# Graph attention on one core: a turn's keys and masks in one transfer each, and a ring of fourteen quads instead of fifteen

## The reference

```python
x_src, x_dst = x[src], x[dst]
for r in range(5):
    mask = edge_types == r
    q = einsum('eh,khd->ekd', x_dst, W_Q[r])      # 100000 x 8 x 16
    k = einsum('eh,khd->ekd', x_src, W_K[r])
    v = einsum('eh,khd->ekd', x_src, W_V[r])
    logits = (q * k).sum(-1) / scale + attn_bias[r]
    # softmax over the edges of this type with the same dst
    attn = segment_softmax(where(mask, logits, NEG), dst)
    out += segment_sum(attn[:, :, None] * v, dst)
out = out @ out_proj_w.T + out_proj_b
h = layernorm(out + x) * ln_gamma + ln_beta
return layernorm(x + h)
```

## Time and profile before

| | us |
|---|---|
| median of 3 runs | 1296.82 (1294.86 to 1297.39) |
| profiled execution, from first to last instruction | 1301.8 |
| DVE busy | 1002.1 (77%) |
| PE busy | 938.5 (72%) |
| POOL busy | 763.0 (59%) |
| ACT busy | 547.3 (42%) |
| mean granted clock of PE, share of full speed | 0.546 |
| DMA | 209.26 MB, mean 161 GB/s |

### The profile page before, as it was taken

How to read it: one execution, slowest core, us unless ns; L and a number is a source line. 1 busy time by engine, 2 the same in 40 slices (tenths; PEclk the granted TensorE clock), 3 DMA queues, 4 the chain that set the end, 5 groups by cost and what they waited for, 6 DMA issues and landing times.

```text
span 1301.8 us, 19088 instructions
## 1 busy us (share of the span) xinstructions
PE 938.5 (72%) x5180; PEld 827.1 (64%) x5180; DVE 1002.1 (77%) x1851; ACT 547.3 (42%) x1044; POOL 763.0 (59%) x859
## 2 busy tenths in 40 slices
PE   9924467866778767877787776877677677666777
PEld 4513456765667656766676765767576666666677
DVE  3656678877878778878878788887788788778996
ACT  5624443444434444444444444444444334343322
POOL 0067666666666666666666666666666666666640
PEclk9956555555555555555555555555555555555555
DMA  8976555554655555555654555655555455555410
GB/s 318 379 216 180 168 159 172 157 160 144 166 159 156 148 157 167 157 139 166 174 161 145 146 164 157 182 140 152 162 168 148 136 140 155 146 141 154 131 48 12
DMA packets 121376, 209.26 MB, mean 161 GB/s; under 512 B 22845, under 2 KB 79546, under 8 KB 121166
## 3 DMA queue, kind: packets, MB, share of 16 engines
q0 software_dynamic: 37632, 102.81, 27.8%
q1 hardware_dynamic: 79602, 92.61, 23.8%
q10 hardware_dynamic: 4032, 12.57, 2.5%
HBM read 176.92 MB, written 30.99 MB: 160 GB/s over the span
## 4 chain that ended last, share of the span: by engine, by line
DVE 36%; issue 28%; another core or an unknown queue 16%; PE 14%; ACT 2%; DVEq 2%; DMA 1%; ACTq 0%; POOL 0%; POOLq 0%; SPq 0%
DVE LT L1324 6%; DVE pool L1416 4%; PE pp L1863 4%; DVE av L666 4%; DVE pool L1387 4%; DVE pool L1288 3%; PE pp L572 3%; DVE pool L1310 2%; PE pp L1807 2%; DVE Tt L1300 2%; DVE Yt L1373 2%; DVE ohn L650 2%; PE pp L1846 2%; DVE Mt L1402 2%
## 5 line engine op out<-in xcount | busy, mean ns | idle before, releaser
L1699 POOL DMA_INDIRECT ring<-KVtab,kvi x784 | 745.6, 951 | 491.0 <-issue 207.3
L1807 PE MATMUL pp<-qwin,pool 128*128 128x128 bf16 x2352 | 293.5, 309 | 73.5 <-issue 53.4
L1863 PE MATMUL pp<-ohn,av 128*128 128x32 f32 x1464 | 328.1, 392 | 20.6 <-issue 18.5
L1863 PEld LDWEIGHTS pp<-ohn,av 128*128 128x128 f32 x1464 | 324.4, 328 | 22.1 <-issue 18.7
L1807 PEld LDWEIGHTS pp<-qwin,pool 128*128 128x128 bf16 x2352 | 262.9, 151 | 112.9 <-issue 111.4
L1310 DVE TENSOR_TENSOR pool<-pp,ring 128x512 f32<-128x512 f32 x196 | 133.5, 681 | 81.9 <-remote 67.3
L909 ACT ACTIVATE Et<-pool 120x512 f32<-120x512 f32 (+1 forms) x66 | 41.6, 630 | 293.2 <-DVE pool L1288 160.5
L1884 PE MATMUL pp<-pool,negb 128*128 128x512 bf16 (+1 forms) x84 | 37.3, 444 | 169.2 <-ACT pool L897 107.4
L882 ACT ACTIVATE pool<-rkb,npid 128x512 bf16<-128x512 bf16 x196 | 139.4, 711 | 36.2 <-DMA rkb<-Ktab 18.9
L1846 PEld LDWEIGHTS pp<-sel,pool 120*128 120x128 f32 (+1 forms) x536 | 129.5, 326 | 38.5 <-issue 38.4
L666 DVE TENSOR_TENSOR av<-ring,pp 128x512 f32<-128x512 f32 x183 | 124.2, 679 | 34.2 <-remote 34.0
(11 more groups left out here) (133 smaller groups left out, 969.1 us busy)
## 6 DMA issues: line engine op xcount, KB each, us to landing
rkb<-Ktab SPq DMA_DIRECT2D x196, 128.0 KB
mk<-Mtab SPq DMA_DIRECT2D x201, 100.2 KB
qwin<-Qfast SPq DMA_DIRECT2D x196, 96.0 KB
KVtab<-pool SPq DMA_DIRECT2D x25, 640.0 KB, 6.3
ring<-KVtab,kvi POOLq DMA_INDIRECT x784
Qfast<-pool ACTq DMA_DIRECT2D x21, 480.0 KB
Qfast<-ring SPq DMA_DIRECT2D x4, 480.0 KB
xs<-in_x_b SPq DMA_DIRECT2D x5, 320.0 KB
```

Of the source, the lines that this page charges most:

```text
L1699: e.indirect_dma_start(kv[:, home(m), j, :], None, KV, bass.IndirectOffsetOnAxis(kvi[:, 4 * q + j:4 * q + j + 1], 0)).then_inc(kv_in[m % 6 ...
L1807: last = e.matmul(pp[2 + m % 2][:, j * C:(j + 1) * C], ohr[:, m % OR, j * C:(j + 1) * C], qwin[:, m % 3, k * C:(k + 1) * C], start=(k == 0 ...
L1863: last = e.matmul(sums_at(f)[:, 0:n], weighed_at(f)[:, j, :], hot_at(f)[:, j, 0:n], start=(j == 0), stop=(j == 3))
```

## The change

- Keys: `load_keys(i)` fetches the rows of all quads of turn i in one transfer, into one of two buffers of three rows each (before: one row, one of three). It is issued in SP's step of the last quad of turn i-2 and waits until ACT has read that one (`KEYS_IN`). ACT waits for the turn's transfer.
- Masks: `load_masks(i)` fetches the masks of the three streams in one transfer. Its source has three dimensions, stream, 40 copies, and the row. All waits for masks count 16 instead of 48.
- The ring: `KR` is 14 instead of 15. Gathers wait for the weighing of quad m-14.
- `pad`, a temporary of the setup in the ring's space, shares its place with the first columns of `natd`, which has been read by then.

```diff
-KR = 15
+KR = 14
...
+def quads_of(i):
+    return [m for m in range(NQ) if turn_of(m)[0] == i]
+
+
+KEYS_IN = {quads_of(i - 2)[-1]: i for i in range(2, NW)}
...
-        pad = temp.take([2, 512], F32, HQ)
         differ = temp.take([2, MROW], F32, HQ)
         junk = natd.bitcast(F32)
+        pad = junk[:, :, 0:512]
...
-        rkb = sb("rkb", [128, 3, 512], BF16)
+        rkb = sb("rkb", [128, 2, G, 512], BF16)
...
-            def load_keys(m):
-                if m == 0:
+            def load_keys(i):
+                if i == 0:
                     e.wait_ge(rk_stored, 2 * 16)
-                if m >= 3:
-                    e.wait_ge(keys_dist, m - 2)
-                q = quad_of(m)
-                e.dma_start(rkb[:, m % 3, :], RK[q:q + 1, :].partition_broadcast(128)).then_inc(rk_in[m % 3], 16)
+                n = len(quads_of(i))
+                if i >= 2:
+                    e.wait_ge(keys_dist, quads_of(i - 2)[-1] + 1)
+                e.dma_start(rkb[:, i % 2, 0:n, :],
+                            RK[i:i + (n - 1) * STREAM + 1:STREAM, :].partition_broadcast(128)).then_inc(rk_in[i % 2], 16)
...
-                for g in range(G):
-                    q = STREAM * g + i
-                    e.dma_start(mk[g * R * H:(g + 1) * R * H, i % MR, :, :].rearrange("p e k -> p (e k)"),
-                                MT[q:q + 1, :].partition_broadcast(R * H)).then_inc(mask_in[i % MR], 16)
+                e.dma_start(mk[:, i % MR, :, :].rearrange("p e k -> p (e k)"),
+                            MT[i:i + 2 * STREAM + 1:STREAM, None, :].broadcast_to([G, R * H, 2 * MROW])).then_inc(
+                                mask_in[i % MR], 16)
...
-            for m in range(3):
-                load_keys(m)
+            for i in range(2):
+                load_keys(i)
...
-                if s + 3 < NQ:
-                    load_keys(s + 3)
+                if s in KEYS_IN:
+                    load_keys(KEYS_IN[s])
...
             def keys(m):
-                e.wait_ge(rk_in[m % 3], 16 * (m // 3 + 1))
+                i, g = turn_of(m)
+                e.wait_ge(rk_in[i % 2], 16 * (i // 2 + 1))
...
-                e.activation(ab[:, :], rkb[:, m % 3, :], ACT.Abs, bias=npid[:, 0:1]).then_inc(keys_dist, 1)
+                e.activation(ab[:, :], rkb[:, i % 2, g, :], ACT.Abs, bias=npid[:, 0:1]).then_inc(keys_dist, 1)
```

More of the change, by code:

```diff
@@ L529, in build @@
         kv_in = sems("kv_in", 6)
-        rk_in, keys_dist, onehot = sems("rk_in", 3), sem("keys_dist"), sem("onehot")
+        rk_in, keys_dist, onehot = sems("rk_in", 2), sem("keys_dist"), sem("onehot")
         qwin_in, tq_stored, xq_in = sems("qwin_in", 3), sems("tq_stored", 2), sems("xq_in", 2)
@@ L916, in put_masks @@
             def put_masks(i):
-                e.wait_ge(mask_in[i % MR], 48 * (i // MR + 1))
+                e.wait_ge(mask_in[i % MR], 16 * (i // MR + 1))
                 e.wait_ge(full_sum, TOTAL[i - 1])
@@ L1378, in forward @@
                 e.wait_ge(turned, i + 1 if i < LASTW else i + 2)
-                e.wait_ge(mask_in[i % MR], 48 * (i // MR + 1))
+                e.wait_ge(mask_in[i % MR], 16 * (i // MR + 1))
                 if i == LASTW:
-                    e.wait_ge(mask_in[(i + 1) % MR], 48 * ((i + 1) // MR + 1))
+                    e.wait_ge(mask_in[(i + 1) % MR], 16 * ((i + 1) // MR + 1))
                 if i >= 3:
```

## The result

The changed kernel takes 1360.11 us (median of four, 1355.07 to 1362.19), the kernel before 1296.49 (four, 1294.86 to 1297.39): 1.0487 times, interval 1.0466 to 1.0509, so 63.6 us more. The prediction was 1326, range 1292 to 1342: right sign, and 34 us short. A ratio with an interval is taken from runs repeated side by side and can differ by up to 0.3% from the quotient of the two medians beside it.

What follows compares the result with a forecast made beforehand. POOL's rhythm of gathers, 784 at 1.496 us, was taken to bound the kernel. Ring +29, keys, masks and start 0 on the 1301.8 us span gave 1330.8, less 5.0 for the runs' median 1326; range 1292 to 1342.

Steps and rivals of the forecast that it cites:

- What bounds the kernel: Whole kernel: POOL's 784 gathers at 1.496 us set the time; PE's results are seen about 2 us after the last gather.
- The ring: POOL's gathers wait for weigh(m-14), which at some group starts cannot come before the release: +29 us, ends 0 and 42.
- my own sum over the 96 group starts: POOL's group starts: new weighing's end plus 0.28 us, less the gather's start; 42 positive, largest 1.99, together 31.6 us.
- Keys: Key loads: ACT's 18.9 us of waits mostly go, but releases do not wait for ACT: 0, at most -18.9 us.
- Masks: Mask loads: issued some 45 us ahead of their scan, so hidden, as is SyncE's issuing: 0 us.
- start: SyncE's loads ahead of the first gathers: 2.3 us of cover for quad 0's window of queries; 0, ends -1 and +1.
- rival of the crowded engines: Mask transfer runs on three engines, first query window after 81, POOL stands 5 to 11 us: 1331 to 1337; chance 0.15.
- The sum: Whole kernel: 29 + 0 + 0 + 0 on the span of 1301.8 gives 1330.8, less 5.0 for the runs' median: 1326.
- Faster: POOL's gathers shorten with fewer SyncE issues: -10 us, 1287 with the ring's wait covered; sign two quads under 11.9; chance 0.15.
- covered: Ring's wait costs nothing as PE's work sets the rhythm: no change, 1297 (1294 to 1299); chance 0.18.
- the second rival: The case covered: PE's true work sets the rhythm, so a gather 0.6 us late has 15 us of cover; chance 0.18.

Runs made afterwards that it cites:

- the standstill: Kind of run in which POOL stands still after every second quad; the kernel before takes 1282 us (first 1296) with it, 1109 us without.
- the first pair: The whole change against the kernel before, as first measured, of the kind with the standstill: 1360.11 against 1296.49 us, 1.0487.

## Why the prediction was right or wrong

**What bounds the kernel: right in the main.** That a later gather delays the end is borne out: the last gather starts 55 us later, in a span 51.5 us longer, and fewer gathers give back time, though 0.76 us each and not 1.50. The sentence that PE's results are seen only 2 us after POOL's last gather was too general. Of DVE's idle times over 1.5 us between the first turns and the last gather, 37 of 59 end 1.7 to 2.6 us after a row's last gather in the kernel before, 32 of 58 in the changed one, and 1 of 16 where the fourth gathers are left out. What I didn't know is that the standstill is a condition of the run: without it a gather costs 1.256, not 1.496.

**The ring, +29 us (0 to 42): the mechanism right, the size too small.** The mechanism is the one that I named, that the weighing cannot come before the release. One term of its sum is wrong: I let POOL go on 0.28 us after the weighing's end, a figure taken from another release, and it goes on 0.74 us after it, at all of the 70 places. With 0.74 in place of 0.28, my own sum over the 96 group starts is 51.4 us instead of 31.6. (Where POOL's wait for `q_expanded` is left out, it follows by 0.27.) The distribution was off as well: I held 1.99 us for the largest delay, and the traces have standstills of up to 7.8 instead of 2.3, since a row that ends ahead of a turn's scan makes POOL wait for the scan too. Alone, in another set, the ring measured +33 (26 to 41), so by that my 29 looks good; but there what the wait costs varies from run to run, as shown below under the sum.

**Keys, 0: right within 4 us where it was measured, without the standstill**, and ACT's waits for them went, as forecast. What I missed is that this part matters for the next.

**Masks, 0 (and start 0, -1 to +1): this is the step whose mechanism failed.** I priced the transfer by its own reader: issued some 45 us ahead of its scan, it was hidden. It was. But it slows what is issued behind it: the first window of queries by 8.5 to 10.4 us, where I had 2.3 us of cover, and later keys and windows. POOL's quad 3 started 8.0 us later for it. Alone, the masks' part costs 14.5 us with the standstill. My rival of the crowded engines had the place (window after 81), the start (5 to 11) and, as far as packets in flight show it, the mechanism, at a chance of 0.15, and then said that later the cover holds; without the standstill that is refuted: POOL stands 43.4 us beyond its usual pauses in the masks alone (my sum over all gathers), 9.6 of it at the start. Its sum, 1331 to 1337, is still 23 us under what was measured.

**The sum.** By the ratios, 33 and 15 make 48 us in the set where both were taken, and the whole measured 46 (38 to 55) in another: with the standstill the parts add up. In the first pair it was 64. The rest lies in the ring's wait. The two traces of the changed kernel, spans of 1353.3 and 1313.5, have 70 standstills each that end with the weighing; from quad 14 on these hold 152 us beyond the usual pause in the first and 109 in the second, all others 75 and 74. The spread of the runs says the same: with the ring of 14 four runs lie 7 to 22 us apart, with the ring of 15, POOL's pacing wait and all gathers at most 5.4. So in the first pair the ring cost some 49 us (an estimate: 63.6 less the masks' 15 of another set), near the 51.4 of the mended sum. The miss of 34 us is then some 20 in the ring's term and some 15 in the masks'. Why the ring's wait costs more in one set than in another isn't settled.

**Faster, and covered: neither.** The sign that I gave for faster, two quads in under 11.9 us, was a bad one: 10 of the changed kernel's 35 rows of two quads took 11.8 to 11.9, and 3 of 84 before, while on average two quads took 12.6 us against 12.0. And the cover of 15 us that the second rival needed isn't there with the standstill, while without it the ring is indeed covered (+1.8 us).

## What to carry to other kernels

Price a transfer by what is issued behind it, not only by who reads it: three rows of masks in one transfer ran with at most six packets in flight, for 6 to 7 us a turn, and the harm was in the keys and query windows issued behind it. Of the two shapes tried here, an outermost dimension of 40 was good and one of three was not; and if such a transfer can't be avoided, issuing it behind what the start waits for should spare the start (not tried). Read how fast an engine goes on from the very kind of release that is meant: 0.46 us too little, at 44 places, made 20 us. A ring that is one slot shorter costs nothing while its consumer keeps up, and 2.6% where the consumer is released only by the producer's pause: look at how far behind the release the freeing instruction stands. Measure both kernels in one set, and more than once: the same pair gave 4.9, 3.6 and 1.5%.

## What the runs showed of the hardware

- One and the same program ran at 1109 us in three sets and at 1282 to 1297 in three others, on one chip (14) in both ways. In traces of the slower kind DVE runs dry towards the end of a row of indirect DMAs: in the kernel before it is busy for 0.35 of the second microsecond after POOL's last gather, and for 0.9 from the fourth on. POOL's own gather is as long (0.95) in both. Which condition picks it wasn't found.
- In that regime the kernel without the pacing wait, with rows of mostly 12 gathers instead of 8, took 12.4% longer.
- POOL goes on 0.74 us after the end of the DVE instruction that it waits for where `q_expanded` is waited for first, and 0.27 us after it where that wait is left out (all 80 standstills of that trace).
- One transfer of 120 rows with three as its outermost dimension: 6.3 to 7.2 us with at most four to six packets in flight; the same bytes in three transfers of 40 rows: 2.1 to 3.4 us with 12 or 13.
- SP's issue of a load behind such a transfer took longer: the two of xqT 5.9 to 6.9 us in six traces with one mask transfer a turn, 0.99 behind nine transfers of 40 rows (in the kernel with three). Nine transfers with three outermost took SP 13.85 us to issue, nine of 40 rows 3.36.
